# A two-layer transformer on one core: its beginning rebuilt (order of loads, banks of the first row's products, norm ahead of modulation, rope keys by ScalarE)

## What is computed

```
def reference(...):
    x = L0_attn_x                                   # (4, 512, 128)
    mod = (_silu(L0_c) @ L0_wmod).reshape(4, 6, 1, -1)
    sa, ca, ga, sb, cb, gb = (mod[:, j] for j in range(6))
    ga, gb = (sign(g) * max(|g|, 0.25) for g in (ga, gb))
    h = _layernorm(x) * (1 + ca) + sa
    x = x + ga * _L0_attn_ref(h, W_kv_down, W_k_up, W_v_up, W_q, W_q_rope, W_k_rope, W_o)
    h = _layernorm(x) * (1 + cb) + sb
    x = x + gb * _L0_ffn_ref(h, ...)                # 15 routed experts, top 3, and a shared one
    ...                                             # layer 1: the same frame, other attention and experts

def _L0_attn_ref(x, ...):                           # causal, 16 heads of 8, with 32 rope dimensions shared by the heads
    c_kv = x @ W_kv_down
    k_rope = _rotary_apply(c_kv @ W_k_rope, cos, sin)
    k, v, q = c_kv @ W_k_up, c_kv @ W_v_up, x @ W_q
    q_rope = _rotary_apply(x @ W_q_rope, cos, sin)
    scores = (q k^T per head + q_rope k_rope^T) / sqrt(40)
    return softmax(causal(scores)) v @ W_o
```

## Time and profile before

| | |
|---|---|
| median of 3 runs | 984.76 us (979.02 to 986.0) |
| the profiled execution as timed | 984.84 us |
| its span | 983.1 us |
| PE busy | 792.4 us (81%) |
| DVE busy | 649.1 us (66%) |
| ACT busy | 524.2 us (53%) |
| POOL busy | 344.6 us (35%) |

### The profile page before, as it was taken

The page is one execution under the profiler, slowest core; times in us unless marked ns, Lnnn a source line. Parts: engine busy times, 40 slices in busy tenths (PEclk is TensorE's granted clock), DMA queues, the critical chain, the costliest instruction groups (busy, mean ns, idle before and its releaser), DMA issues. The chain is left out here.

```text
span 983.1 us, 12967 instructions
## 1 busy us (share of the span) xinstructions
PE 792.4 (81%) x4212; PEld 497.0 (51%) x4212; DVE 649.1 (66%) x1290; ACT 524.2 (53%) x970; POOL 344.6 (35%) x389
## 2 busy tenths in 40 slices
PE   3547888988898889999989899789989888527850
PEld 2233444555454667787767544345344444227740
DVE  3135568676663777776768696488898876347853
ACT  1013454545556677776757456456656656217740
POOL 3413775543532000000005345653453542133425
PEclk9987999999999999999999979899999999659985
DMA  4251331102110490000002112210110200011013
GB/s 125 48 95 21 85 81 35 34 22 46 30 24 2 137 285 6 1 1 1 1 8 57 43 42 63 60 35 17 38 25 18 58 4 10 4 54 56 32 34 84
DMA packets 56414, 44.75 MB, mean 46 GB/s; under 512 B 6598, under 2 KB 47387, under 8 KB 56347
## 3 DMA queue, kind: packets, MB, share of 16 engines
q1 hardware_dynamic: 55323, 41.82, 16.8%
q0 software_dynamic: 1024, 2.10, 0.7%
...
## 5 line engine op out<-in xcount | busy, mean ns | idle before, releaser
L926 ACT ACTIVATE ring<-single 128x512 f32<-128x512 f32 (+3 forms) x512 | 253.1, 517 | 226.3 <-PE single L1176 218.8
L1554 DVE TENSOR_REDUCE mneg<-pair 128x2 f32<-128x1024 f32 (+3 forms) x256 | 258.5, 1022 | 87.7 <-PE pair L1160 33.2
L1176 PE MATMUL single<-q_op,k_op 104*128 104x512 f32 (+3 forms) x512 | 216.5, 443 | 17.8 <-ACT ring L926 9.2
L1156 PE MATMUL pair<-k_op,q_op 96*128 96x512 f32 (+3 forms) x512 | 172.1, 415 | 42.2 <-DVE mneg L1554 22.6
L786 POOL TENSOR_SCALAR k_op<-k_stk,cst 104x512 fp32r<-104x512 f32 x64 | 100.0, 1577 | 276.2 <-DMA k_stk<-hl 258.5
L1176 PEld LDWEIGHTS single<-q_op,k_op 122*128 122x128 f32 (+1 forms) x512 | 97.9, 197 | 98.6 <-ACT ring L926 72.6
L1156 PEld LDWEIGHTS pair<-k_op,q_op 120*128 120x128 f32 (+1 forms) x512 | 98.9, 207 | 86.8 <-DVE mneg L1554 44.8
L1192 PE MATMUL p_o<-ring,vaug 128*9 128x512 f32 (+3 forms) x1024 | 116.1, 526 | 1.0 <-ACT ring L926 0.9
L721 POOL TENSOR_SCALAR_AFFINE_SELECT ring<-ring 128x256 f32<-128x256 f32 x128 | 52.3, 408 | 149.4 <-ACT ring L926 149.2
L955 ACT ACTIVATE ring<-pair,cols 128x512 f32<-128x512 f32 x136 | 86.1, 685 | 33.8 <-PE pair L1236 27.5
L1600 DVE TENSOR_TENSOR ring<-ring,single 128x1024 f32<-128x1024 f32 x60 | 73.3, 1221 | 45.5 <-ACT ring L955 44.4
...
## 6 DMA issues: line engine op xcount, KB each, us to landing
...
q_op<-hl SPq DMA_DIRECT2D x96, 64.0 KB, 2.0
...
k_op<-hl SPq DMA_DIRECT2D x48, 64.0 KB
k_stk<-hl SPq DMA_DIRECT2D x48, 64.0 KB, 2.0
...
```

The source lines that it names most:

```text
L926: exp_done.by(act.activation(ring[:, n % 8, lo:T], singles[n % 2][:, lo:T], ACT.Exp), (L, n))
L1156: ins = pe.matmul(both[:, i, 0:hi], r32(qs[:, P * qt:P * (qt + 1)]), r32(ks[:, 0:hi]), start=i == 0 or L == 1 or qt >= 2, stop=L == 1)
L1176: st_full.by(pe.matmul(singles[n % 2][:, lo:T], r32(ks[:, P * kc:P * (kc + 1)]), r32(qs[:, lo:T]), start=True, stop=True), (L, n))
L1554: s_taken.by(dve.tensor_reduce(mneg[:, G % 2, 2 * p:2 * p + 2, qt], both[:, :, 0:hi], axis=AX.X, op=ALU.max, negate=True), (L, m))
```

## The change

The lead and the loads are reordered; the work itself is the same.

- Loads: row 0 of x is issued second. Group 3 keeps only the four weights for the absorbed product; `W_q`, `W_q_rope` and the bf16 constants are group 5. The modulation table of layer 0 (group 2) comes between them, that of layer 1 is group 6. Rows 1 to 3 of x and `W_o` are group 4 and issued ahead of the first expert pieces. The experts' second biases and router tables are group 7, issued behind the first maxima's DMAs and two expert pieces. The second layer's attention weights are group 8, issued in two halves within stage 1.
- Row 0's products have banks of their own: `rp` singles[0], `q` singles[1], `rs` and `k` the two pairs. `q` and `k` wait only for `ln1`, `rs` for `rp`.
- VectorE norms row 0 ahead of and around the columns and silu. The modulation is split by layer: layer 0's is a copy and an add ahead of the row's products, the rest (the guards of all gates, the zeroing of `p_o`) comes with layer 1's, behind the products. On TensorE layer 0's modulation comes behind the absorbed product, layer 1's behind `v`.
- Row 0's rope rows: q's by SP, between q's and k's head rows; k's are issued by ScalarE, which also copies them into `k_op0` for the first three head groups, behind `v`. GpSimd copies q's.
- `mt0` of the first group stands behind unit 7 and no longer behind unit 8.

```
@@ -359,6 +359,8 @@
     before = dict(zip(misc[1:], misc))
+    before[("q", 0)] = before[("k", 0)] = ("ln1", 0)
+    before[("rs", 0)] = ("rp", 0)
...
@@ -432,8 +434,11 @@
 
+    first_bank = {("rp", 0): singles[0][:, :], ("q", 0): singles[1][:, :], ("rs", 0): pairs[0][:, 0, :], ("k", 0): pairs[1][:, 0, :]}
     def bank(part):
-        return singles[0] if part in in_units else p_m
+        return first_bank[part] if part in first_bank else singles[0] if part in in_units else p_m
@@ -456,19 +461,21 @@
         load(0, cst[:, :], a["const"][:, 0:C_N])
+        load(1, x[:, 0, :, :], a["L0_attn_x"][0].rearrange("(t p) d -> p t d", p=P))
...
             load(0, rows[r:r + src.shape[0], :], src)
-        load(1, x[:, 0, :, :], a["L0_attn_x"][0].rearrange("(t p) d -> p t d", p=P))
-        for L in range(2):
-            load(2, w_mod[:, L, :, :], a[f"L{L}_wmod"].rearrange("d (j n) -> d j n", j=6))
         for dst, name in ((raw[:, P:2 * P], "W_kv_down"), (raw[:, 2 * P:3 * P], "W_k_up"), (rhs_abs[:, P:2 * P], "W_v_up"),
-                          (rhs_abs[:, 2 * P:2 * P + DR], "W_k_rope"), (raw[:, 0:P], "W_q"), (w_rope[:, 0:DR], "W_q_rope")):
+                          (rhs_abs[:, 2 * P:2 * P + DR], "W_k_rope")):
             load(3, dst, a[f"L0_attn_{name}"])
-        load(3, raw_bf[:, :], a["const"][:, C_N:C_N + 3 * P])
+        load(2, w_mod[:, 0, :, :], a["L0_wmod"].rearrange("d (j n) -> d j n", j=6))
+        for dst, name in ((raw[:, 0:P], "W_q"), (w_rope[:, 0:DR], "W_q_rope")):
+            load(5, dst, a[f"L0_attn_{name}"])
+        load(5, raw_bf[:, :], a["const"][:, C_N:C_N + 3 * P])
+        load(6, w_mod[:, 1, :, :], a["L1_wmod"].rearrange("d (j n) -> d j n", j=6))
@@ -503,18 +510,22 @@
                 rope_set.wait_ge(sp, 4 * r - 2)
-            for w in range(2):
+            if r == 1:
+                sp.wait_ge(rope_k, 3)
+                apart(sp)
+            for w in range(2 if r else 1):
...
 
-        def head_dma(G):
+        def head_dma(G, which=(0, 1)):
...
                 exp_done.wait_ge(sp, (0, 16 * (G - 3) + 15))
-            elif G == 0:
+            elif G == 0 and 1 in which:
...
                 apart(sp)
-            for w, part in enumerate(("q", "k")):
+            for w in which:
+                part = ("q", "k")[w]
@@ -542,35 +553,40 @@
 
+        for b in range(1, NB):
+            load(4, x[:, b, :, :], a["L0_attn_x"][b].rearrange("(t p) d -> p t d", p=P))
+        load(4, w_out[0][:, :], a["L0_attn_W_o"])
...
             expert0(n)
+        head_dma(0, (0,))
         rope_dma(0)
-        for G in range(3):
+        head_dma(0, (1,))
+        for G in (1, 2):
             head_dma(G)
+        m_dma(0, 0)
...
         expert0(3)
-        m_dma(0, 0)
-        sp.wait_ge(mod_full, 1)
-        apart(sp)
-        for b in range(1, NB):
-            load(4, x[:, b, :, :], a["L0_attn_x"][b].rearrange("(t p) d -> p t d", p=P))
-        sp.wait_ge(pool_set, 1)
-        apart(sp)
-        load(4, w_out[0][:, :], a["L0_attn_W_o"])
         for q in range(0, P, 16):
-            load(4, b_2[q:q + E0, :], a["L0_ffn_rb2"])
-            load(4, b_2[q + E0:q + 16, :], a["L0_ffn_sb2"])
+            load(7, b_2[q:q + E0, :], a["L0_ffn_rb2"])
+            load(7, b_2[q + E0:q + 16, :], a["L0_ffn_sb2"])
         for L, (rw, rb) in enumerate((("L0_ffn_gW", "L0_ffn_gb"), ("L1_ffn_Wr", "L1_ffn_br"))):
-            load(4, w_rt[L][:, :], a[rw])
-            load(4, b_rt[L][:, :], a[rb].partition_broadcast(P))
-        n_g, gi, go = a["L1_attn_w_qkv"].shape
-        for g in range(n_g):
-            load(4, w_qkv[gi * g:gi * (g + 1), go * g:go * (g + 1)], a["L1_attn_w_qkv"][g])
-            load(4, w_out[1][gi * g:gi * (g + 1), gi * g:gi * (g + 1)], a["L1_attn_w_proj"][g])
+            load(7, w_rt[L][:, :], a[rw])
+            load(7, b_rt[L][:, :], a[rb].partition_broadcast(P))
+        def second_layer(lo, hi):
+            n_g, gi, go = a["L1_attn_w_qkv"].shape
+            for g in range(n_g * lo // 2, n_g * hi // 2):
+                load(8, w_qkv[gi * g:gi * (g + 1), go * g:go * (g + 1)], a["L1_attn_w_qkv"][g])
+                load(8, w_out[1][gi * g:gi * (g + 1), gi * g:gi * (g + 1)], a["L1_attn_w_proj"][g])
...
             head_dma(G + 3)
+            if r == 1:
+                sp.wait_ge(pool_set, 1)
+                apart(sp)
+                second_layer(0, 1)
@@ -583,6 +599,8 @@
             m_dma(0, G + 3)
+            if r == 1:
+                second_layer(1, 2)
@@ -653,6 +671,7 @@
         pool.tensor_copy(rhs_abs[:, 2 * P + DR + half:2 * P + 2 * DR], rhs_abs[:, 2 * P:2 * P + half]).then_inc(pool_set, 1)
+        pool.wait_ge(loads[5], n_load[5])
@@ -678,7 +697,7 @@
             ins = pool.tensor_copy(r32((q_op0, k_op0)[w][0:96, at:at + 2, :]), qk_rope[:, w:w + 1, :].broadcast_to([96, 2, T]))
-            if (w, half) == (1, 1):
+            if (w, half) == ((1, 1) if G >= 3 else (0, 1)):
...
@@ -721,8 +740,8 @@
         for G in range(3):
-            for w, half in ((0, 0), (0, 1), (1, 0), (1, 1)):
-                rope_copy(G, w, half)
+            for half in range(2):
+                rope_copy(G, 0, half)
@@ -876,6 +895,10 @@
                 hi_ready.by(act.activation(r32(rope_hl[:, 0, :]), src[0:64, :], ACT.Copy), key)
+                if s == 0:
+                    taken.wait_ge(act, key)
+                    for t in range(3):
+                        act.dma_start(qk_rope[DR * t:DR * (t + 1), 1, :], rope_hl[DR:2 * DR, TERM[1][t], :]).then_inc(rope_rows, 16)
@@ -1026,6 +1049,14 @@
                 part(name, b)
+            if L == 0:
+                act.wait_ge(rope_rows, R_ROWS)
+                apart(act)
+                for G in range(3):
+                    for at in (GH * G, GH * G + 2):
+                        ins = act.activation(r32(k_op0[0:96, at:at + 2, :]), qk_rope[:, 1:2, :].broadcast_to([96, 2, T]), ACT.Copy)
+                    ins.then_inc(rope_k, 1)
+                act.wait_ge(mod_ready, 2)
@@ -1046,16 +1077,19 @@
         pe.transpose(singles[0][:, 0:P], raw[:, P:2 * P], ident).then_inc(kvd_full, 1)
-        pe.wait_ge(silu_ready, 1)
-        pe.wait_ge(loads[2], n_load[2])
-        for L in range(2):
+        pe.wait_ge(kvd_ready, 1)
+        pe.wait_ge(pool_set, 2)
+        pe.matmul(singles[1][:, 0:320], kvdT[:, :], rhs_abs[:, :], start=True, stop=True).then_inc(abs_full, 1)
+        def modulation(L):
...
                 ins = pe.matmul(p_o[:, n:n + NB], w_mod[:, L, j, :], silu[:, 0, NB * L:NB * (L + 1)], start=True, stop=True)
-        ins.then_inc(mod_full, 1)
-        pe.wait_ge(kvd_ready, 1)
-        pe.wait_ge(pool_set, 2)
-        pe.matmul(singles[1][:, 0:320], kvdT[:, :], rhs_abs[:, :], start=True, stop=True).then_inc(abs_full, 1)
+            ins.then_inc(mod_full, 1)
+        pe.wait_ge(silu_ready, 1)
+        pe.wait_ge(loads[2], n_load[2])
+        modulation(0)
@@ -1082,7 +1116,7 @@
             elif name == "lg":
-                pe.wait_ge(loads[4], n_load[4])
+                pe.wait_ge(loads[7], n_load[7])
@@ -1123,6 +1157,8 @@
                          "wo0": modT[:, 0, 2, :], "wo1": modT[:, 1, 2, :]}[name]
+                if name == "wo0":
+                    pe.wait_ge(mod_ready, 2)
@@ -1140,6 +1176,8 @@
                     rope_set.wait_ge(pe, G if G % NG < 3 else G - 1)
+                    if G < 3:
+                        pe.wait_ge(rope_k, G + 1)
@@ -1215,9 +1253,12 @@
                 part(name, b)
+            if L == 0:
+                pe.wait_ge(loads[6], n_load[6])
+                modulation(1)
...
                 max_unit(L, m)
-                if i == 8:
+                if i == 7:
@@ -1358,13 +1399,16 @@
 
-        dve.wait_ge(cols_full, 1)
-        dve.tensor_copy(cols[:, :], p_m[:, 0:R_N]).then_inc(cols_ready, 1)
-        dve.wait_ge(exp_c, 1)
-        step(dve.tensor_scalar(silu[:, 2, :], silu[:, 1, :], 1.0, None, ALU.add))
-        step(dve.reciprocal(silu[:, 1, :], silu[:, 2, :]))
-        dve.wait_ge(cols_ready, 1)
-        dve.tensor_tensor(silu[:, 0, :], silu[:, 1, :], cols[:, R_C:R_C + 2 * NB], ALU.mult).then_inc(silu_ready, 1)
+        def columns():
+            dve.wait_ge(cols_full, 1)
+            dve.tensor_copy(cols[:, :], p_m[:, 0:R_N]).then_inc(cols_ready, 1)
+        def silu_of_c():
+            dve.wait_ge(exp_c, 1)
+            step(dve.tensor_scalar(silu[:, 2, :], silu[:, 1, :], 1.0, None, ALU.add))
+            step(dve.reciprocal(silu[:, 1, :], silu[:, 2, :]))
+            dve.wait_ge(cols_ready, 1)
+            dve.tensor_tensor(silu[:, 0, :], silu[:, 1, :], cols[:, R_C:R_C + 2 * NB], ALU.mult).then_inc(silu_ready, 1)
@@ -1392,9 +1436,12 @@
 
-        def modulation():
-            dve.wait_ge(mod_full, 1)
-            step(dve.tensor_copy(modT[:, :, :, :].rearrange("p l j b -> p (l j b)"), p_o[:, 0:12 * NB]))
+        def modulation(L):
+            dve.wait_ge(mod_full, L + 1)
```

(25 more changed lines are left out.)

8 lines of the change are left out of this document (4 added, 4 removed).

## The result

Before, the median is 984.68 us (979.02 to 986.0, four runs), after **955.79 us** (951.16 to 958.02, four runs): a ratio of 0.9709, with a 95% interval of 0.9682 to 0.9735. The forecast was 955, with a range of 948 to 963. The profiled executions took 984.84 and 951.16 us as timed, with spans of 983.1 and 949.4.

The account below looks back on a forecast made before the run. No engine but two chains of waits, the lead and VectorE's stall, were taken to bound the first 80 us. Gains of 8.5+4.4+1.3+13.3+2.2 = 29.7 from 984.8 gave 955 us, range 948 to 963.

Parts of the forecast that it names:

- T: End of hT, row 0's modulated input: 15.2 instead of 23.71 by load order and norm, gain 8.5 us (7.0 to 9.5).
- Own banks to the first reduction: From hT's end to VectorE's first score reduction: T+18.6 instead of T+23.05, gain 4.4 us (3.0 to 5.5).
- Rival 1: TensorE's clock rises within the lead, so rs, k and v run fast: 4.2 us less, 951 us; chance 0.16.
- VectorE's whole block (3.05 us): VectorE's part of the second layer's modulation, ahead of its first score reduction: put at 3.05 us.
- rival 2: ScalarE's queue becomes the bound, its issues and copies costing say 1.0 and 1.6 us: 959 us; chance 0.18.
- Maxima to the first exponent: First reduction to the first exponents' product, 14.4 us before: gain 1.3 us (0 to 2.5), product at T+31.6 = 46.8.
- Stall and clock: VectorE's wait ahead of the second batch-row norm goes, 13.3 us; TensorE's clock doesn't fall behind it, 2.2 us.
- Rival 4: Another wait holds the norm of row 1, so 13.3+2.2 us stay: 970 us; chance 0.04.
- Late loads: SP's 20 issues of b_2 and router tables and the second layer's 16, moved later: no effect, zero.
- The gain passes to the end in full: Everything behind the first quads is relative to them, so the whole 29.7 us reaches the kernel's end.
- Rival 3: TensorE stays at 1.2 GHz into the attention, making the kernel slower than before: 990 us; chance 0.02.

Follow-up runs that it names:

- second_loads_back: The changed kernel with the second layer's 16 attention loads back ahead of the attention's second transfer of maxima: 957.44 us, ratio 0.972.
- both: The changed kernel with GpSimd filling the ones rows first and the second modulation's products ahead of the value product: 952.78 us, ratio 0.9699.
- before_rows_early: The kernel before with only rows 1 to 3 of x and W_o issued ahead of its attention, in their own group: 968.88 us, ratio 0.9848.
- experiment 6: The same run as second_loads_back: the changed kernel with the second layer's 16 attention loads back behind the router tables, 957.44 us, ratio 0.972.

## Why the prediction was right

By its own steps, T = 14.60:

- **T**: put at 15.2 (gain 8.5), measured 14.60 (9.1). The norm starts at 5.35 and ends its small steps by 9.65, where 5.4 and about 11 were put for the whole of it (10.88). Of the 9.1, the loads' order gives 2.3 and the norm's place some 5.2; the rest was not tried alone (the halved modulation, 2.56 us of products less, is the likely owner). *There is luck in this number.* The prediction had GpSimd's fill start near 12.9 and asked only whether it ends before the k rows are wanted. The profiled execution, the shortest of the four, had it at 14.13, behind the add at 13.02 that releases hT. In second_loads_back, whose lead is the same, the fill began at 13.22, the add took 5.29 us, and hT came 4.7 us later. The prediction had no term for this.
- **Own banks to the first reduction**: T+18.6 put, T+18.95 measured, gain 4.1 instead of 4.4. *The sum held because two errors in it cancelled.* Rival 1 came true in part: rs and k ran at 1.07 and 1.12, so k's low part was ready at T+9.2, not T+10.8, and the modulation's products were over at T+13.1, not T+15.5. Against that, the term "VectorE's whole block (3.05 us)" measured 5.8, since GpSimd's copies, which the prediction had placed beside it as harmless, held five of its operations. The 3.05 itself held two such waits: before, the same block had operations of 0.75 and 0.63 us beside GpSimd's fills, and without any it takes 1.95 (both). ScalarE's issues were 0.63 each and its copies 0.97, as put (0.63, 1.06), so rival 2 did not come. The rotated rows landed 3.5 us behind SyncE's last issue of them, not 2.0, with the key rows' transfer beside them (T+12.9 for T+11.7).
- **Maxima to the first exponent**: T+31.6 put, that is 46.8; 46.88 measured, which is T+32.3. The time is right because three small errors cancel: T 0.6 early, the first reduction 0.35 late from T, and from there 13.33 us instead of 13.0 (gain 1.05 instead of 1.3). The maxima's transfer lands 2 us from its second issue, as put.
- **Stall and clock**: 13.3 and 2.2 put, 15.5 together; 15.55 by the ruler, 15.03 alone in before_rows_early, where 13.33 is the stall and 1.7 what is left for the clock, against 2.2. Rival 4 would have left it. In 60 to 100 the granted clock is 1.00.
- **Late loads**: put at zero. The 20 issues end at 54.4 and the next wanted transfer is issued at 58.36. Moving the second layer's was worth some 1 us, as experiment 6 shows.
- **The gain passes to the end in full**: 29.8 at 57 us, 30.35 at 273 and 31.5 at 791, of which the last microsecond came behind layer 0's attention. In the medians it is 28.9; 0.9 less is within what falls of the clock add or take.
- **Rivals 1 and 3**: of rival 1 (951 us) only rs and k came, 2.0 us of product time, and part of v (1.50 us); the clock fell within v, and the eight units ran slow. Rival 3 (TensorE slow into the attention) did not come: the clock was back near 52, 5 us into the quads.
